# Part of layer 3's edge sort moved on VectorE, from layer 1's graph passes into the loop of layer 1's expert mixture

## Chip, cores and metric

The kernel runs on one core of a Trainium2 chip. The metric is the device time in microseconds (us). Before the change the median of three runs is 3659.58 us, the lowest 3652.49 and the highest 3664.68. The engines are named as in the profile: PE is TensorE, DVE is VectorE, ACT is ScalarE, POOL is GpSimd and SP is SyncE.

## What is computed

Four layers run on 3125 nodes with 256 features and 50000 edges. Each layer is a graph part and then a feed-forward part. Three of these parts touch the change:

```python
# layer 1, graph part: four graph convolutions, one after another
h = relu(gcn_conv(x, src, dst, W1, b1, n)); z = relu(gcn_conv(h, src, dst, W2, b2, n))
h = relu(gcn_conv(z, src, dst, W3, b3, n)); x_hat = gcn_conv(h, src, dst, W4, b4, n)
# layer 1, feed-forward: 16 experts, the two best for each node
topk_vals, topk_idx = top_k(x @ gate_w + gate_b, 2)
moe = sum(softmax(topk_vals) * expert_out[topk_idx]); y = layernorm(x + moe) * gamma + beta
# layer 3, graph part: it needs the edges grouped by key (tile of the target, leading or not)
x = x + L3_gnn(layernorm(x), weight, bias, edge_index, edge_type_8)
```

## The kernel before

The nodes lie in T = 25 tiles of 125 rows. Layer 1's graph part (`layer1_gnn`, L1820) makes four passes over 25 blocks of the edge-count matrix. SP loads a block or finds it resident, ACT casts it to 16 bits (L2007), PE multiplies it (L1924), and DVE scales the product and splits it into parts (L2039 to L2094). After each block DVE calls `sort.step(dve, p * T + j)`, which is one small step of `EdgeSort` (L2127). That class prepares layer 3's edges, in 392 columns by 128 partitions and 30 keys, with a counting sort:

- In pass 0 the keys, their totals and the offsets are made (steps 5 to 14).
- A **rank** (L2256 to L2263) handles one key with four operations on 128x392: a comparison, a scan, a multiply-add and an add into `pos`. Ten ranks run at steps 15 to 24 of pass 0, and twenty at steps 75 to 94, which are 20 of the 25 blocks of pass 3.
- A **tiles** operation (L2252) on 1x420 counts, for one key, which tiles of the sorted table start behind it. The thirty of them run at steps 25 to 54, that is after every block of pass 1 and after the first five of pass 2.
- The **last steps** (L2266 to L2291, at step 96) turn tiles and positions into tables and rows.

`scatter` (L2293) is what uses the rows. POOL runs it only after layer 1.

Beside all this, POOL adds layer 2's edge weights into a matrix in memory, column by column: 391 indirect transfers that add (`add_weight`, L1288, issued at L1296). The first 258 (`BEFORE_EXPERTS`) come before the expert mixture, the others in it and after it. Layer 2 starts with loads from that matrix.

Layer 1's expert mixture (`layer1_ffn`, L2660) sorts the 6250 node-expert pairs into 64 blocks of 128 rows. A barrier (`stage`, L94, its wait at L106) stands ahead of its loop. In the loop POOL gathers the rows of a block (L2787), eight blocks ahead. PE turns them (L2845) and multiplies them twice (L2853, L2876). DVE adds the bias (L2913, the "y add"), and POOL scatters the result (L2801). After 56 of the 64 blocks, all but every eighth, POOL also issues one weight add:

```python
for n in range(SLOTS):
    pool.wait_ge(x_turned, n + 1)
    if n + ROWS < SLOTS + 2:
        gather(n + ROWS)
    pool.wait_ge(y_put, n + 3)
    pool.indirect_dma_start(out=g.moe[:, :], ..., in_=ys[:, n % AHEAD, :], ...)
    if n in beside:
        add_weight(nc, g, pool, BEFORE_EXPERTS + FIRST + beside.index(n))
```

DVE has nothing else in that loop than one addition of beta to all of `X` ahead of the first block (L2905) and the 64 y adds. PE waits at block n for y add n - 2, whose place in PSUM it writes again. The order on every engine is the order in which the code is written.

Of the kernel before, what the change touches and what calls it, by code (L numbers as in the profile page):

```python
# [2126 lines left out]
class EdgeSort:  # L2127
# [3 lines left out]

    KEYED, TOTALS, OFFSETS, RANKS, ROWS = 5, 7, 14, [*range(15, 25), *range(75, 95)], 96

# [6 lines left out]
    def signals(self, ctx):  # L2140
        _, _, sem = bufs(self.nc, ctx, "sort")
        self.cleared, self.loaded, self.blank, self.filled, self.counted, self.summed, self.placed = (
            sem(m) for m in ("cleared", "loaded", "blank", "filled", "counted", "summed", "placed"))

    def rooms(self, sub, sums):
        sb, _, _ = bufs(self.nc, sub, "sort")
        self.raw = sb("raw", [128, 3, ET], I32)
        self.key, self.pos, self.pad = self.g.cell_id, self.g.cell_off, self.g.trash
        self.tmp, self.hot, self.run, self.one = (sb(m, [128, ET]) for m in ("tmp", "hot", "run", "one"))
        self.each = sb("each", [128, 5, ET], BF16)  # L2150
        self.tiles, self.padrow = sb("tiles", [1, ST]), sb("padrow", [128, 1])
        self.leads = self.raw[0:1, :, :].rearrange("p k t -> p (k t)")[:, 0:ST].bitcast(F32)
        self.total, self.nt, self.ends, self.starts, self.off = (
            sb(m, [128, KEYS]) for m in ("total", "nt", "ends", "starts", "off"))
        self.sums = sums

    def load(self, sp, a):
# [9 lines left out]
    def clear(self, dve):  # L2167
# [7 lines left out]
        nc.vector.memset(self.one[:, :], 1.0)  # L2175
        nc.vector.memset(self.tiles[:, :], -1.0)
        dve.drain()
# [19 lines left out]
    def step(self, dve, i):  # L2197
# [40 lines left out]
        if i == self.OFFSETS:  # L2238
# [10 lines left out]
                                           op0=ALU.mult, op1=ALU.add)  # L2249
            dve.drain()  # L2250
        if T <= i < T + KEYS:
            nc.vector.scalar_tensor_tensor(out=self.tiles[:, :], in0=g.iota[0:1, :], scalar=starts[0:1, i - T:i - T + 1],  # L2252
                                           in1=self.tiles[:, :], op0=ALU.is_ge, op1=ALU.add)
# [11 lines left out]
        if i == self.ROWS:  # L2265
# [4 lines left out]
            nc.vector.tensor_scalar(self.leads[:, :], self.leads[:, :], -1.0, 2.0, ALU.mult, ALU.add)  # L2270
            dve.drain()
            nc.vector.tensor_scalar(self.tiles[:, :], self.tiles[:, :], -float(LEADING), None, ALU.add)
            nc.vector.tensor_copy(g.levels[0:1, :], self.leads[:, 0:RING])
            dve.drain()
            nc.vector.tensor_copy(g.kmap[0:1, :], self.tiles[:, :])
            nc.vector.tensor_scalar(tmp[:, :], pos[:, :], 1.0 / 128, -63.5 / 128, ALU.mult, ALU.add)
            dve.drain()
            self.round(dve, tmp[:, :])
            nc.vector.scalar_tensor_tensor(out=pos[:, :], in0=tmp[:, :], scalar=-128.0, in1=pos[:, :],
                                           op0=ALU.mult, op1=ALU.add)  # L2280
# [3 lines left out]
            nc.vector.tensor_scalar(pad[:, :], pad[:, :], self.padrow[:, :], None, ALU.mult)  # L2284
            dve.drain()
            for c in range(EC + 1, ET):
                nc.vector.tensor_scalar(pad[:, c:c + 1], pad[:, c:c + 1], float(128 * (c - EC)), None, ALU.add)
# [371 lines left out]

def layer1_ffn(nc, g, a):  # L2660

# [6 lines left out]
    with ExitStack() as ctx:  # L2668
        sb, ps, sem = bufs(nc, ctx, "f1")
        logits, chosen, weight = sb("logits", [128, T, NE]), sb("chosen", [128, T, 2]), sb("weight", [128, T, 2])  # L2670
        posf = sb("posf", [128, 2 * T])
# [92 lines left out]
        with ExitStack() as sub:  # L2764
# [136 lines left out]
            @block.vector  # L2901
            def _(dve):
                dve.sem_inc(y_put, 2)
                dve.wait_ge(affine_loaded, 32)
                nc.vector.tensor_tensor(g.X[0:P], g.X[0:P], wide(beta[0:P, :], P, T, D), ALU.add)  # L2905
                for i in range(BODIES):
                    for j in range(AHEAD):
                        n = AHEAD * i + j
                        dve.wait_ge(b_loaded[j], (i + 1) * 16)
                        if i:  # L2910
                            dve.wait_ge(stored[j], i * 16 + stored_before[j])
                        dve.wait_ge(y_made, n + 1)
                        nc.vector.tensor_tensor(ys[:, j, :], pY[:, j % 2, 0:D], b[:, j, :], ALU.add).then_inc(y_put, 1)  # L2913

        with ExitStack() as sub:
# [737 lines left out]
def build(nc, a, out):  # L3653
    with ExitStack() as ctx:
        def sb(name, shape, dt=F32):
            return ctx.enter_context(nc.sbuf_tensor(name, shape, dt))
# [52 lines left out]
        sort = EdgeSort(nc, g, keep)  # L3709
        kept = keep.enter_context(ExitStack())  # L3710
        csb, _, _ = bufs(nc, kept, "cells")
        g.cell_id, g.cell_off, g.trash = (csb(m, [128, ET]) for m in ("id", "off", "trash"))
        g.cell_count = csb("count", [128, ET], U16)
# [20 lines left out]
        with ExitStack() as early:  # L3734
            NE, _, F = a["L1_ffn_w1"].shape
            g.w2 = early.enter_context(nc.sbuf_tensor("w2", [128, NE * F // 128 * D], F32))
            layer1_ffn(nc, g, a)
        clear_semaphores(nc, g)
# [31 lines left out]
```

## Time and profile before

| | us |
|---|---|
| median of 3 runs (lowest, highest) | 3659.58 (3652.49, 3664.68) |
| span of the profiled execution | 3782.6 |
| PE busy in it | 2772.2 (73%) |
| POOL busy | 2338.7 (62%) |
| DVE busy | 1733.1 (46%) |
| ACT busy | 916.1 (24%) |
| mean granted TensorE clock | 0.845 |

The profiled execution gives no time but its span, which is 123 us above the median of the runs without a profile. Times in its trace count from the span's start. The part that the change touches lies between 864 us (start of layer 1's pass 0) and 1835 us (the last weight add). A busy share of the whole span says little about it: pass 3 and the expert loop have different bounds.

### The profile page before, as it was taken

To read this page: it belongs to the slowest core of one execution; us is meant where nothing else is said; L and a number is where in the kernel's file an instruction comes from. 1 tells how busy PE (TensorE), PEld (TensorE's weight loads), DVE (VectorE), ACT (ScalarE), POOL (GpSimd) and SP (SyncE) were. 2 spreads that over 40 slices of the span, in tenths; PEclk is the share of its full clock that TensorE was granted. 3 is DMA by queue.
4 is the path that set the end of the run, shared out by engine and by line. 5 is a ranking of instruction groups with operands and counts; after the bars stand their busy time and mean duration, and the time that the engine had idled before them with its cause. 6 is when DMAs were issued, how large, how long until landed. Compare 5 with 4: busy or idle time off the path is not lost.

```text
span 3782.6 us, 57993 instructions
## 1 busy us (share of the span) xinstructions
PE 2772.2 (73%) x20290; PEld 2148.5 (57%) x20291; DVE 1733.1 (46%) x4547; ACT 916.1 (24%) x2203; POOL 2338.7 (62%) x1884
## 2 busy tenths in 40 slices
PE   3778446728989849871699989989996444446897
PEld 2556425627988848761588878855543223225565
DVE  7996765325766650017111122234443444446344
ACT  4654221125674403323111100022110000001121
POOL 6788888887888877778665566610016667661332
PEclk9767677769999859995899999989998767767899
DMA  8655222226785748773445533311236333336342
GB/s 317 185 154 127 1 1 13 9 1 181 168 213 125 158 92 214 205 207 44 112 138 178 200 107 134 104 34 55 67 103 202 95 92 94 92 89 160 78 134 68
DMA packets 286360, 449.09 MB, mean 119 GB/s; under 512 B 167034, under 2 KB 214887, under 8 KB 272124
## 3 DMA queue, kind: packets, MB, share of 16 engines
q1 hardware_dynamic: 121376, 296.50, 24.7%
q0 software_dynamic: 160256, 104.37, 18.0%
q10 hardware_dynamic: 4464, 44.80, 2.9%
q8 instruction: 153, 2.51, 0.3%
q14 instruction: 111, 0.91, 0.1%
HBM read 319.16 MB, written 125.83 MB: 118 GB/s over the span
## 4 chain that ended last, share of the span: by engine, by line
PE 35%; POOL 8%; DVE 8%; another core or an unknown queue 8%; issue 7%; DMA 3%; DVEq 2%; ACT 1%; SPq 1%; POOLq 0%; ACTq 0%
PE g_acc L2405 12%; POOL weight_cells L1296 8%; PE f2m_pR L3137 5%; DVE X L1387 4%; PE f3e_pH L3591 3%; PE f2m_pR L3109 3%; DMA weight_cells<-added_weight,added_row 3%; PE f1e_pH L2853 3%; PE f3e_pY L3600 2%; PE f1e_pY L2876 2%; DVE g3g_hot L1365 2%; PE f2m_pO L3120 1%; PE g3g_pp L1358 1%; PE g_psL L2389 1%
## 5 line engine op out<-in xcount | busy, mean ns | idle before, releaser
L508 POOL DMA_INDIRECT count_cells<-cells_count,added_row x391 | 643.1, 1645 | 155.4 <-issue 130.6
L1296 POOL DMA_INDIRECT weight_cells<-added_weight,added_row x391 | 635.9, 1626 | 139.1 <-issue 113.7
L2405 PE MATMUL g_acc<-g_H,g_blocks 125*125 125x256 f32 x2500 | 565.2, 385 | 38.3 <-DMA g_blocks<-weight_cells 34.8
L2307 POOL DMA_INDIRECT slots_dram<-sort_rec,sort_row x392 | 378.1, 965 | 262.2 <-DMA slots_dram<-sort_rec,sort_row 124.6
L2405 PEld LDWEIGHTS g_acc<-g_H,g_blocks 125*125 125x125 f32 x2500 | 473.2, 191 | 111.3 <-issue 40.0
L1345 POOL DMA_INDIRECT g3a_got<-relations,g3g_idx x316 | 306.2, 969 | 150.0 <-issue 88.7
L1358 PE MATMUL g3g_pp<-g3a_got,g3g_hot 128*125 128x256 f32 x728 | 233.5, 461 | 224.1 <-DVE X L1387 119.6
L1358 PEld LDWEIGHTS g3g_pp<-g3a_got,g3g_hot 128*125 128x125 f32 x728 | 148.7, 223 | 308.9 <-issue 288.8
L1387 DVE TENSOR_TENSOR X<-X,g3g_pp 125x256 f32 x420 | 176.8, 421 | 300.0 <-DMA f_b<-in_L_ffn_b 191.2
L3292 POOL DMA_INDIRECT g3a_got<-relations,g3a_first x48 | 46.5, 968 | 366.8 <-SPq L3071 345.5
L2007 ACT CAST g_blocks<-g_blocks 128x3125 f16<-128x3125 uint16 x85 | 235.7, 2793 | 101.5 <-DMA g_blocks<-count_cells 96.4
L2472 DVE SCALAR_TENSOR_TENSOR g_tmp<-g_acc,dinv,g_b 125x256 f32<-125x256 f32 x50 | 24.2, 484 | 488.4 <-PE g_acc L2405 285.2
L1113 ACT ACTIVATE X<-same_scores 128x128 bf16<-128x128 f32 (+3 forms) x392 | 166.0, 438 | 113.3 <-PE same_scores L1102 93.0
L3137 PE MATMUL f2m_pR<-f2m_w,f2m_tT 128*125 128x512 f32 x400 | 181.4, 607 | 14.5 <-DVE f2m_ys L3244 11.4
L1924 PE MATMUL g_acc<-XN,g_blocks 125*128 125x64 bf16 (+1 forms) x3750 | 173.8, 207 | 8.5 <-issue 6.9
L1924 PE MATMUL g_acc<-parts,g_blocks 125*128 125x128 bf16 (+1 forms) x3750 | 171.0, 206 | 6.9 <-issue 4.5
L1924 PEld LDWEIGHTS g_acc<-XN,g_blocks 125*128 125x128 f16 x3750 | 167.0, 98 | 14.9 <-issue 11.2
L1924 PEld LDWEIGHTS g_acc<-parts,g_blocks 125*128 125x128 f16 x3750 | 164.2, 98 | 12.3 <-issue 7.5
L2853 PE MATMUL f1e_pH<-f1e_xT,f1e_w 128*128 128x128 f32 x1040 | 132.7, 282 | 26.0 <-issue 15.9
L2853 PEld LDWEIGHTS f1e_pH<-f1e_xT,f1e_w 128*128 128x128 f32 x1040 | 125.3, 195 | 41.5 <-issue 25.9
L2913 DVE TENSOR_TENSOR f1e_ys<-f1e_pY,f1e_b 128x256 f32<-128x256 f32 x64 | 27.2, 425 | 258.9 <-PE f1e_pY L2876 146.4
L1100 PE MATMUL same_scores<-edges_other,edges_own 128*128 128x128 bf16 (+3 forms) x392 | 141.0, 374 | 5.4 <-DMA edges_other<-digits_dram 5.4
(777 smaller groups left out, 5305.4 us busy)
## 6 DMA issues: line engine op xcount, KB each, us to landing
g_blocks<-weight_cells SPq DMA_DIRECT2D x49, 1562.5 KB
g_blocks<-count_cells SPq DMA_DIRECT2D x85, 781.2 KB, 14.2
weight_cells<-edges_stripe ACTq DMA_DIRECT2D x25, 1562.5 KB
f1e_w<-in_L_ffn_w SPq DMA_DIRECT2D x68, 512.0 KB
relations<-f2m_ys SPq DMA_DIRECT2D x25, 896.0 KB
f_w<-in_L_ffn_w SPq DMA_DIRECT2D x16, 1024.0 KB
count_cells<-edges_XT POOLq DMA_DIRECT2D x19, 781.2 KB
f1e_b<-in_L_ffn_b SPq DMA_DIRECT2D x68, 128.0 KB
```

What stands on the lines that cost most here:

```text
L508: pool.indirect_dma_start(out=rows, out_offset=bass.IndirectOffsetOnAxis(ap=g.cell_row[:, t:t + 1], axis=0), in_=g.cell_count[:, t:t + 1], ...
L1113: self.nc.scalar.activation(self.same[:, k % self.SAME, 0:n], self.scores[:, k % self.SCORES, 0:n], ACT.Relu, accum_out=self.found[:, k:k ...
L1296: pool.indirect_dma_start(out=rows, out_offset=bass.IndirectOffsetOnAxis(ap=g.cell_row[:, t:t + 1], axis=0), in_=g.cell_weight[:, t:t + 1] ...
L1345: pool.indirect_dma_start(out=ahead.place(j), out_offset=None, in_=table[:, :], in_offset=bass.IndirectOffsetOnAxis(ap=idx[:, n:n + 1], ax ...
L1358: last = nc.tensor.matmul(pp[0:P, n // 2 % BANKS, half], hot[:, n % HOTS, :], ahead.place(j), start=True, stop=True)
L1387: nc.vector.tensor_tensor(part, part, pp[0:P, n // 2 % BANKS, half], ALU.add).then_inc(added if n % 2 else first_added, 1)
L1924: last = nc.tensor.matmul(acc[:, i % ACCS, 0:WIDTH[p]], blocks[0:P, place(p, j), t * P:t * P + 128], part(p, t, k), start=(t == 0 and k == ...
L2007: nc.scalar.copy(blocks[:, at, 0:N], counts[:, at, 0:N]).then_inc(halved, 1)
L2307: pool.indirect_dma_start(out=g.slots_dram[:, :], out_offset=bass.IndirectOffsetOnAxis(ap=self.row[:, c:c + 1], axis=0), in_=self.rec[:, c ...
L2405: last = nc.tensor.matmul(acc[0:P, i % 3, 0:D], blocks[0:P, i % BLOCKS, t * P:(t + 1) * P], H[p][0:P, t, :], start=(t == 0), stop=(t == T ...
L2853: last = nc.tensor.matmul(pH[:, j % 2, f * 128:(f + 1) * 128], w1[:, j % AHEAD, k, f * 128:(f + 1) * 128], xT[:, j % 2, k * 128:(k + 1) * ...
L3137: last = nc.tensor.matmul(pR[0:P, chunk_place(n), :], tT[:, (t - 1) % 3, k, :], w[:, k, 2 * c:2 * c + 2, :].rearrange("p r n -> p (r n)"), ...
```

## The change

Twenty ranks, thirty tiles operations and the last steps leave the DVE code of the four passes and are called in the DVE loop of the expert mixture instead, each after a y add: a tiles operation after each of the blocks 0 to 29, a rank after each of the even blocks 0 to 38, and the last steps, in five pieces, after the blocks 40 to 44. The ten ranks of pass 0 stay. The buffers move with them: at step 14 the 128x392 rooms (`tmp`, `hot`, `run`, `one`) move into `g.slots`, which is free once it has been written out as a blank (`filled`), with a new memset of `one`. `tiles` and `leads` are allocated in the mixture, where `tiles` is set to -1 ahead of the addition of beta. `starts`, `off` and `padrow` become views of `sort.row`. No transfer and no wait of another engine is added or removed.

```diff
-    KEYED, TOTALS, OFFSETS, RANKS, ROWS = 5, 7, 14, [*range(15, 25), *range(75, 95)], 96
+    KEYED, TOTALS, OFFSETS, RANKS = 5, 7, 14, [*range(15, 25), *range(100, 140, 2)]
+    BESIDE, ROWS = 100, 140
...
+    def last_rooms(self, ctx):
+        sb, _, _ = bufs(self.nc, ctx, "sort")
+        self.tiles, self.leads = sb("tiles", [1, ST]), sb("leads", [1, ST])
...
+    def move_rooms(self, dve):
+
+        dve.wait_ge(self.filled, 16)
+        free = self.g.slots[:, :, :].rearrange("p t f -> p (t f)")
+        self.tmp, self.hot, self.run, self.one = (free[:, k * ET:(k + 1) * ET] for k in range(4))
+        self.nc.vector.memset(self.one, 1.0)
+        dve.drain()
...
-        nc.vector.memset(self.tiles[:, :], -1.0)
...
-            dve.drain()
-        if T <= i < T + KEYS:
-            nc.vector.scalar_tensor_tensor(out=self.tiles[:, :], in0=g.iota[0:1, :], scalar=starts[0:1, i - T:i - T + 1],
+            self.move_rooms(dve)
+        if self.BESIDE <= i < self.BESIDE + KEYS:
+            k = i - self.BESIDE
+            nc.vector.scalar_tensor_tensor(out=self.tiles[:, :], in0=g.iota[0:1, :], scalar=starts[0:1, k:k + 1],
                                            in1=self.tiles[:, :], op0=ALU.is_ge, op1=ALU.add)
...
+        if i == self.ROWS + 1:
             nc.vector.tensor_scalar(self.tiles[:, :], self.tiles[:, :], -float(LEADING), None, ALU.add)
...
+        if i == self.ROWS + 2:
             nc.vector.tensor_scalar(tmp[:, :], pos[:, :], 1.0 / 128, -63.5 / 128, ALU.mult, ALU.add)
...
+        if i == self.ROWS + 3:
             nc.vector.scalar_tensor_tensor(out=pos[:, :], in0=tmp[:, :], scalar=-128.0, in1=pos[:, :],
...
+        if i == self.ROWS + 4:
             for c in range(EC + 1, ET):
...
-def layer1_ffn(nc, g, a):
+def layer1_ffn(nc, g, a, sort):
...
+        sort.last_rooms(ctx)
...
                 dve.sem_inc(y_put, 2)
+                nc.vector.memset(sort.tiles[:, :], -1.0)
+                dve.drain()
                 dve.wait_ge(affine_loaded, 32)
                 nc.vector.tensor_tensor(g.X[0:P], g.X[0:P], wide(beta[0:P, :], P, T, D), ALU.add)
...
                         nc.vector.tensor_tensor(ys[:, j, :], pY[:, j % 2, 0:D], b[:, j, :], ALU.add).then_inc(y_put, 1)
+                        sort.step(dve, sort.BESIDE + n)
+                        dve.drain()
...
-            layer1_ffn(nc, g, a)
+            layer1_ffn(nc, g, a, sort)
+        ranked.close()
```

On DVE in pass 1 before, one block's six operations stand between two tiles operations. `parts` and `g_some` belong to the pass, `sort_` to the sort:

```order
L2252 SCALAR_TENSOR_TENSOR sort_tiles<-iota,sort_starts,sort_tiles 1x420
L2053 SCALAR_TENSOR_TENSOR g_some<-g_acc,dinv,g_b 125x64
L2056 TENSOR_SCALAR g_some<-g_some,dinv 125x64
L2039 CAST parts<-g_some 125x64
L2041 TENSOR_TENSOR g_left<-g_some,parts 125x64
L2043 CAST parts<-g_left 125x64
L2045 TENSOR_TENSOR parts<-g_left,parts 125x64
L2252 SCALAR_TENSOR_TENSOR sort_tiles<-iota,sort_starts,sort_tiles 1x420
```

After the change the six operations of a block follow each other directly, in all 25 blocks of pass 1; the last row here begins the next block:

```order
L2053 SCALAR_TENSOR_TENSOR g_some<-g_acc,dinv,g_b 125x64
L2056 TENSOR_SCALAR g_some<-g_some,dinv 125x64
L2039 CAST parts<-g_some 125x64
L2041 TENSOR_TENSOR g_left<-g_some,parts 125x64
L2043 CAST parts<-g_left 125x64
L2045 TENSOR_TENSOR parts<-g_left,parts 125x64
L2053 SCALAR_TENSOR_TENSOR g_some<-g_acc,dinv,g_b 125x64
```

On DVE at the start of the expert loop before, from the branch into it (L2901) on:

```order
L2901 UNCONDITIONAL_BRANCH
L2905 TENSOR_TENSOR X<-X,f_beta 125x6400
L2913 TENSOR_TENSOR f1e_ys<-f1e_pY,f1e_b 128x256 x64
L110 UNCONDITIONAL_BRANCH
L2932 UNCONDITIONAL_BRANCH
L2938 SCALAR_TENSOR_TENSOR XN<-w,f_weight,XN 125x256 x10
```

So the 64 y adds stand there with nothing between them. The same place after the change, where `slots` holds the moved rooms of the sort and `sort_row` the views of it:

```order
L2919 UNCONDITIONAL_BRANCH
L2922 MEMSET sort_tiles 1x420
L2925 TENSOR_TENSOR X<-X,f_beta 125x6400
L2933 TENSOR_TENSOR f1e_ys<-f1e_pY,f1e_b 128x256
L2264 SCALAR_TENSOR_TENSOR sort_tiles<-iota,sort_row,sort_tiles 1x420
L2268 TENSOR_SCALAR slots<-cells_id 128x392
L2270 SCALAR_TENSOR_TENSOR slots<-slots 128x392
L2272 SCALAR_TENSOR_TENSOR slots<-slots,sort_row 128x392
L2275 TENSOR_TENSOR cells_off<-cells_off,slots 128x392
L2933 TENSOR_TENSOR f1e_ys<-f1e_pY,f1e_b 128x256
L2264 SCALAR_TENSOR_TENSOR sort_tiles<-iota,sort_row,sort_tiles 1x420
L2933 TENSOR_TENSOR f1e_ys<-f1e_pY,f1e_b 128x256
```

So a memset stands ahead of the addition to `X`, five operations follow an even block's y add and one an odd block's.

## Rows read from the trace of the kernel before

**Rows 1.** The page: the span, and the chain that ended last, by line.

```profile
span 3782.6 us, 57993 instructions
...
PE g_acc L2405 12%; POOL weight_cells L1296 8%; PE f2m_pR L3137 5%; DVE X L1387 4%; PE f3e_pH L3591 3%; PE f2m_pR L3109 3%; DMA weight_cells<-added_weight,added_row 3%; PE f1e_pH L2853 3%; PE f3e_pY L3600 2%; PE f1e_pY L2876 2%; DVE g3g_hot L1365 2%; PE f2m_pO L3120 1%; PE g3g_pp L1358 1%; PE g_psL L2389 1%
```

**Rows 2.** Windows table: pass 1, pass 2, pass 3, expert loop (cut inside it).

```profile
core 0: us, PE busy (x) PEld busy (x) DVE busy (x) ACT busy (x) POOL busy (x), PEclk, DMA share, GB/s
1003.00:1072.00 69.00, 60.26 (x1866) 56.59 (x1865) 52.12 (x167) 54.38 (x20) 57.72 (x38) 1.00 0.84 215
1077.00:1168.00 91.00, 81.78 (x2046) 71.99 (x2046) 56.18 (x180) 59.55 (x46) 75.31 (x50) 1.00 0.75 180
1168.00:1291.00 123.00, 120.95 (x1954) 116.36 (x1954) 86.75 (x170) 61.21 (x46) 103.78 (x64) 0.99 0.51 100
...
1412.00:1664.00 252.00, 227.12 (x1509) 202.94 (x1508) 24.64 (x58) 83.40 (x290) 193.64 (x166) 0.99 0.79 209
```

**Rows 3.** Timeline, DVE in pass 1: start us, duration us, engine, line, operation.

```profile
1016.53 0.65 DVE L2252 SCALAR_TENSOR_TENSOR sort_tiles<-iota,sort_starts,sort_tiles 1x420 f32<-1x420 f32 x1
...
1019.33 0.65 DVE L2252 SCALAR_TENSOR_TENSOR sort_tiles<-iota,sort_starts,sort_tiles 1x420 f32<-1x420 f32 x1
```

**Rows 4.** Timeline, ACT in pass 1: its last cast of a count block.

```profile
1062.66 2.80 ACT L2007 CAST g_blocks<-g_blocks 128x3125 f16<-128x3125 uint16 x1 [0.70 <-DMA g_blocks<-count_cells]
```

**Rows 5.** Timeline, PE: the last matmuls of pass 1's last block.

```profile
1072.18 0.25 PE L1951 MATMUL g_acc<-g_heavy_rows,heavier_target_hot 128*128 128x64 bf16 x3
```

**Rows 6.** Timeline, DVE in pass 3: one rank and the next block's first operation.

```profile
1200.95 0.36 DVE L2256 TENSOR_SCALAR sort_hot<-cells_id 128x392 f32<-128x392 f32 x1
1201.39 0.98 DVE L2258 TENSOR_TENSOR_SCAN sort_run<-sort_one,sort_hot 128x392 f32<-128x392 f32 x1
1202.44 0.63 DVE L2260 SCALAR_TENSOR_TENSOR sort_run<-sort_run,sort_off,sort_hot 128x392 f32<-128x392 f32 x1
1203.14 0.57 DVE L2263 TENSOR_TENSOR cells_off<-cells_off,sort_run 128x392 f32<-128x392 f32 x1
1204.17 0.29 DVE L2069 COPY g_u<-g_acc 125x128 f32<-125x128 f32 x1 [0.46 <-PE g_acc L1951]
```

**Rows 7.** Timeline, POOL at the expert loop's start.

```profile
1391.63 1.01 POOL L2787 DMA_INDIRECT f1e_xs<-table,f_node  x1 [11.92 <-DVEq L106]
1392.94 6.48 POOL L2787 DMA_INDIRECT f1e_xs<-table,f_node  x1 [0.30 <-issue]
1399.73 0.95 POOL L2787 DMA_INDIRECT f1e_xs<-table,f_node  x1 [0.30 <-issue]
```

**Rows 8.** Timeline, DVE at the expert loop's start.

```profile
1391.75 6.83 DVE L2905 TENSOR_TENSOR X<-X,f_beta 125x6400 f32<-125x6400 f32 x1 [0.42 <-DVEq L106]
...
1417.20 0.42 DVE L2913 TENSOR_TENSOR f1e_ys<-f1e_pY,f1e_b 128x256 f32<-128x256 f32 x1 [4.05 <-PE f1e_pY L2876]
```

**Rows 9.** Timeline, POOL inside the expert loop: one block's three transfers.

```profile
1504.33 0.99 POOL L2787 DMA_INDIRECT f1e_xs<-table,f_node  x1 [0.30 <-PE f1e_pT L2845]
1505.63 0.97 POOL L2801 DMA_INDIRECT moe<-f1e_ys,f_to  x1 [0.30 <-issue]
1506.91 1.61 POOL L1296 DMA_INDIRECT weight_cells<-added_weight,added_row  x1 [0.31 <-issue]
```

**Rows 10.** Timeline, POOL in pass 3, beside the rank of rows 6.

```profile
1199.91 1.54 POOL L1296 DMA_INDIRECT weight_cells<-added_weight,added_row  x1 [0.30 <-issue]
1201.76 1.96 POOL L1296 DMA_INDIRECT weight_cells<-added_weight,added_row  x1 [0.30 <-issue]
```

**Rows 11.** Groups by line, POOL, pass 3 while it holds ranks (1169.5 to 1268 us).

```profile
L1296 POOL DMA_INDIRECT weight_cells<-added_weight,added_row x51 | 83.9, 1645 | 15.6 <-issue 14.0 <-DMA weight_cells<-added_weight,added_row 1.5
```

**Rows 12.** Groups by line, POOL, pass 1 (1003 to 1072 us).

```profile
L1296 POOL DMA_INDIRECT weight_cells<-added_weight,added_row x38 | 60.1, 1581 | 11.6 <-issue 10.7 <-DMA weight_cells<-added_weight,added_row 0.9
```

**Rows 13.** Waits table, POOL in the expert loop (1412 to 1690): us, times, longest.

```profile
POOL moe L2801 <- DVE f1e_ys L2913: 11.9, 11, 1.6
```

**Rows 14.** Timeline, POOL: the last of layer 1's adds.

```profile
1832.96 1.55 POOL L1296 DMA_INDIRECT weight_cells<-added_weight,added_row  x1 [0.30 <-issue]
```

More of the change, by code:

```diff
@@ L2150, in rooms @@
         self.each = sb("each", [128, 5, ET], BF16)
[L2151 to L2154, printed above, removed]
+        self.total, self.nt, self.ends = (sb(m, [128, KEYS]) for m in ("total", "nt", "ends"))
+        free = self.row[:, :].bitcast(F32)
+        self.starts, self.off, self.padrow = free[:, 0:KEYS], free[:, KEYS:2 * KEYS], free[:, 2 * KEYS:2 * KEYS + 1]
         self.sums = sums
+    def move_rooms(self, dve):
[4 more added lines that the diff above has]
+        dve.drain()
     def load(self, sp, a):
@@ L2913, in _ @@
                         nc.vector.tensor_tensor(ys[:, j, :], pY[:, j % 2, 0:D], b[:, j, :], ALU.add).then_inc(y_put, 1)
+                        sort.step(dve, sort.BESIDE + n)
+                        dve.drain()
         with ExitStack() as sub:
@@ L3709, in build @@
         sort = EdgeSort(nc, g, keep)
-        kept = keep.enter_context(ExitStack())
+        ranked = keep.enter_context(ExitStack())
+        csb, _, _ = bufs(nc, ranked, "cells")
+        g.cell_id, g.cell_off, g.trash = (csb(m, [128, ET]) for m in ("id", "off", "trash"))
+        kept = ranked.enter_context(ExitStack())
         csb, _, _ = bufs(nc, kept, "cells")
-        g.cell_id, g.cell_off, g.trash = (csb(m, [128, ET]) for m in ("id", "off", "trash"))
         g.cell_count = csb("count", [128, ET], U16)
```

## Prediction

> **What bounds the kernel now.** I read the chain of the page first. Layer 1's part of it is POOL's column of weight adds, L1296, with 8% of the span, followed by layer 2's g_acc [rows 1]. The last add begins at 1832.96 us [rows 14], and layer 2 begins by loading the matrix that the adds fill. So whatever moves POOL's end moves the time, about us for us. Next I read the windows table by stage, because the change touches three stages with different limits. In pass 1 neither PE (60.26 of 69 us) nor DVE (52.12) is full, in pass 3 PE is (120.95 of 123), and in the expert loop DVE is nearly idle (24.64 of 252) while POOL is not (193.64 busy, and it pays 0.30 of issue ahead of each of its 166 transfers, 50 us more) [rows 2]. Last I read the timelines. In the loop a block costs POOL three transfers, 0.99 + 0.97 + 1.61 us, and three times 0.30, so 4.47 us [rows 9]. The y add waited 4.05 us and took 0.42, so it comes every 4.47 us too [rows 8]. POOL sets the pace in the loop. Ahead of the loop it does not: its first gather waited 11.92 us for the barrier, which DVE ended [rows 7]. So time saved in the passes does reach the loop's start, as long as POOL has its 258 adds done, and time lost on POOL in the loop reaches the end.
>
> **The change, part by part.** The sum is made in the profiled execution, whose span of 3782.6 us is 123 us above the median of the runs; terms of a few us are taken over unscaled.
>
> *Tiles out of pass 1.* A tiles operation costs DVE 0.65 us and about 0.07 behind it. Where DVE runs back to back, a block takes it 1019.33 - 1016.53 = 2.80 us with it and would take 2.08 without [rows 3]. PE needs 60.26 / 25 = 2.41 us a block [rows 2], so DVE would no longer be behind PE. What remains is the count blocks: the last one is cast at 1062.66 + 2.80 = 1065.46 [rows 4], and one block of PE behind that is 1067.87. Before, PE's last block ended at 1072.43 [rows 5], so 4.6 us can be gained at most here. The least is nothing, if PE's end hangs on the casts in a way that these rows don't show. I take -4, nearer to the upper end, since DVE's excess is seen in every block of the first half.
>
> *Tiles out of pass 2.* Five operations, 0.72 us each. PE was busy 81.78 of 91 us and DVE 56.18 [rows 2], so DVE has room: 0, at best -3.6.
>
> *Ranks and last steps out of pass 3.* A rank is 0.36 + 0.98 + 0.63 + 0.57 us and some 0.3 of drains, 2.86 us [rows 6], and twenty leave. But behind one DVE waited 0.46 us for PE [rows 6], and PE idled only 2.05 us of the pass [rows 2]. PE's matmuls hide the ranks: 0, at best -2. POOL's adds lose their stalls here, but POOL then only waits longer than 11.92 us at the barrier.
>
> *The move of the rooms.* One memset on 128x392 in pass 0, of the size of the comparison's 0.36 us, behind a wait for a write that was issued blocks earlier: 0, bounds 0 and +0.7.
>
> *The memset of tiles ahead of the addition to X.* It and its drain start that addition later. An addition of 6.83 us to all of X runs at the loop's start [rows 8], and the second gather beside it took 6.48 us where the next took 0.95 [rows 7]. PE's first block hangs on these gathers. The addition moves by about one operation on one partition, 0.4 us, and the gather with it: +0.4, bounds 0 and +0.7.
>
> *DVE in the loop.* An even block now costs 0.42 + 0.72 + 2.86 = 4.00 us, an odd one 1.14, against 4.47 between y adds. It fits, by half a microsecond: 0. If that cover went, the next y add would be late, and with it POOL's scatter behind it on POOL's queue, then the next weight add.
>
> *POOL beside the ranks.* This is the price that decides. While a rank's last addition ran from 1203.14 to 1203.71 [rows 6], a weight add that began at 1201.76 did not end before 1203.72: it took 1.96 us instead of 1.54 [rows 10]. In pass 3's stretch with twenty ranks the 51 adds took 1645 ns on the mean [rows 11], so 51 x 0.105 = 5.4 us too long, 0.27 us a rank. There POOL began a transfer every 98.5 / 51 = 1.93 us. In the loop it begins three in 4.47, one per 1.49, so there are 1.3 times as many to hit: 0.35 us a rank, 7.0 for twenty. Tiles operations: in pass 1 the 38 adds took 1581 ns [rows 12], 38 x 0.041 = 1.6 us too long for 25 of them, 0.06 each; times 1.3, thirty cost 2.4. The last steps I count as two ranks, 0.7. That is 10.1 us of stalls. POOL also waits in the loop, 11.9 us in 11 waits for a y add [rows 13], around the blocks 0, 8, 16 and so on that have no weight add. Of the twenty ranks five stand at such a block, so I take a quarter off: +7.6. Bounds: 0 if POOL's waits swallow all of it, and 20 x (0.63 + 0.57) = +24 if every rank costs POOL both its operations on two inputs.
>
> **Sum:** -4 + 0.4 + 7.6 = +4.0 us, about **3663.5 us**. A measurement of this kernel tells some 0.3% (11 us) from no change, so this is no change.
>
> **Rivals.**
> *Slower: the stalls lock to the blocks.* In the passes POOL and DVE drift past each other, and 0.27 is a mean over all positions. In the loop the y add follows the gathers that POOL issues, so a rank stands at the same place against POOL's three transfers in each block, and it can be a bad one. If each of twenty ranks costs its last addition, 0.57, and every second tiles operation its whole 0.65, that is 11.4 + 9.8 + 0.7 + 0.4 - 4 = +18, so 3678 us. It decides from about 0.7 us per even block on. For it: the y adds and POOL show the same period [rows 8, 9]. Against it: POOL's slack at every eighth block, and no add in rows 10 lost more than 0.42.
> *Faster: the passes give all and the loop takes nothing.* -4.6 in pass 1, -3.6 in pass 2, -2 in pass 3 and stalls that vanish in POOL's 11.9 us of waits: -10, about 3650 us. For it: the 11.92 us at the barrier lets a gain through. Against it: PE's full pass 3, and that each part must give its upper bound.
> *The move out of the passes is worth nothing.* If pass 1 hangs on its loads (the last cast waited 0.70 us for one [rows 4]), the gain is 0 and the stalls stay: +8, 3667.5 us, still inside what can't be told.
> *Only the comparison stalls POOL.* The addition to X reads two inputs from the core's memory, and the gather beside it was held for 6.48 us [rows 7, 8]; the trace so speaks for stalls by such operations. If they didn't stall POOL in the loop, a rank would hold it only by its comparison, 0.36 us once in 1.49 of POOL's starts and for half of it, 0.04 us: below 1 us for twenty, a sum of -2.7 and 3657 us. The Trainium skill, "SBUF — State Buffer", section "Who interferes with whom", says that an operation with two SBUF inputs takes only the read side of the port that GpSimd shares, and infers that it should not hold up the generation of descriptors, where a fast one-input operation does. By that rule the sum would be this rival's; rows 7 and 8 speak against it here, so I give it little.
>
> **How the numbers follow.** My own case with the last two rivals beside it: 0.60 (forecast 0.47, nothing from the passes 0.08, comparison only 0.05), from 3655 to 3670. Locked stalls: 0.25. All gains: 0.15. The range leaves out about one in ten on each side and goes from 3649, the full gain, to 3679, the locked case. Within 0.3% is 3648.6 to 3670.6, so same is 0.60, slower 0.25 and faster 0.15.
>
> **What would show it.** In the profile after, pass 1 should end about 4 us earlier against pass 0's end, pass 3 should still take 121 us with PE full, and POOL's wait at the barrier should grow from 11.92. In the loop transfers of POOL beside a rank should be 0.3 to 0.5 us longer, ending when a DVE operation ends, and the last add should start about as late as before. The forecast is wrong if the loop grows by more than 15 us, or if its transfers keep 0.99, 0.97 and 1.61 us beside the ranks.

## The result and the profile after

The change makes the kernel a little slower. The median goes from 3655.48 to 3665.16 us (twenty runs each), and the ratio is 1.0023 with a 95% interval of 1.0016 to 1.003. That is 9.7 us by the medians and 8.4 by the ratio (6 to 11 by its interval). It is less than the 0.3% at which the forecast drew its line, but with twenty runs the interval leaves 1 out: it is a small loss, not none. The forecast was 3663.5 us, in a range of 3649 to 3679.

The page after the change, its span and its chain by line:

```profile
span 3664.6 us, 58012 instructions
...
PE g_acc L2422 15%; POOL weight_cells L1296 12%; POOL g3a_got L1345 6%; PE f2m_pR L3159 5%; PE f3e_pH L3613 3%; PE f2m_pR L3131 3%; PE f3e_pY L3622 3%; DMA weight_cells<-added_weight,added_row 2%; PE f2m_pO L3142 1%; DMA g3a_got<-relations,g3g_idx 1%; PE g_psL L2406 1%; PE g3g_pp L1358 1%; POOL moe L2819 1%; POOL f1e_xs L2805 1%; PE f1e_pH L2871 1%
```

POOL's weight adds now hold 12% of the chain, where [rows 1] had 8%. But the span of [rows 1] is 3782.6 us and this one 3664.6, and most of that difference lies behind layer 1, where the change does nothing. The first profiled execution was an unusual one. So the kernel before was profiled once more, and what follows compares with that second execution (span 3652.0 us).

> The kernel before, unchanged, for a second profiled execution: the first one spans 3782.6 us and its stages behind layer 1 can't be set beside those after the change. Theory A (POOL's stalls in the expert loop make the loss): in an ordinary execution the last weight add ends 5 to 10 us earlier than after the change, counted from pass 0's first matmul, and the later stages agree to 1 or 2 us. Theory B (the loss arises behind layer 1): from pass 0's first matmul to the last weight add it takes about 963 us as in the first profile, 6 us more than after the change, and a later stage is some 15 us shorter.

It measured 3653.73 us. From pass 0's first matmul to the end of the last weight add it took 948.7 us, and after the change 957.2: 8.6 us more, as theory A expected, while theory B's 963 did not come again. Behind that add the two executions differ by 3.3 us (1831.4 and 1834.7), more than the 1 or 2 that theory A allowed; in the profiled executions below this stretch goes from 1834 to 1842 us, so a single trace can't place a few us there.

POOL by line over its whole expert loop, from the first gather to the last scatter, in this second execution of the kernel before (columns: instructions | busy us, mean ns | idle ahead of them and what ended it):

```profile
L1296 POOL DMA_INDIRECT weight_cells<-added_weight,added_row x58 | 93.3, 1608 | 17.7 <-issue 16.5 <-DMA weight_cells<-added_weight,added_row 0.9 <-DVE f1e_ys L2913 0.3
L2787 POOL DMA_INDIRECT f1e_xs<-table,f_node x66 | 70.7, 1070 | 24.3 <-issue 18.0 <-DVEq L106 4.5 <-PE f1e_pT L2845 1.2
L2801 POOL DMA_INDIRECT moe<-f1e_ys,f_to x64 | 62.4, 975 | 19.5 <-issue 17.7 <-DVE f1e_ys L2913 1.2 <-PE f1e_pT L2845 0.3
```

The same for the kernel after the change:

```profile
L1296 POOL DMA_INDIRECT weight_cells<-added_weight,added_row x58 | 95.4, 1644 | 17.7 <-issue 17.1 <-DMA weight_cells<-added_weight,added_row 0.6
L2805 POOL DMA_INDIRECT f1e_xs<-table,f_node x66 | 76.3, 1156 | 29.9 <-issue 17.4 <-DVEq L106 10.1 <-PE f1e_pT L2863 2.1
L2819 POOL DMA_INDIRECT moe<-f1e_ys,f_to x64 | 66.6, 1041 | 19.5 <-issue 18.0 <-DVE f1e_ys L2933 1.2 <-DMA weight_cells<-added_weight,added_row 0.3
```

The same 188 transfers took 93.3 + 70.7 + 62.4 = 226.4 us before and 95.4 + 76.3 + 66.6 = 238.3 after: 11.9 us more. The loop, from the first gather's start to the last scatter's end, went from 283.3 to 295.2 us, by the same 11.9. Nothing was absorbed in the loop, since in both kernels POOL idled almost only for issue: it waited 1.2 us for y adds, not the 11.9 of [rows 13]. The gathers grew most, from 1070 to 1156 ns.

Where the loop begins, in the second execution of the kernel before (timeline of POOL):

```profile
1387.18 1.01 POOL L2787 DMA_INDIRECT f1e_xs<-table,f_node  x1 [4.53 <-DVEq L106]
1388.49 6.49 POOL L2787 DMA_INDIRECT f1e_xs<-table,f_node  x1 [0.30 <-issue]
```

And after the change:

```profile
1387.08 1.01 POOL L2805 DMA_INDIRECT f1e_xs<-table,f_node  x1 [10.07 <-DVEq L106]
1388.39 7.08 POOL L2805 DMA_INDIRECT f1e_xs<-table,f_node  x1 [0.30 <-issue]
```

The first gather starts at the same time. POOL waits longer for the barrier, 10.07 instead of 4.53 us, because the passes no longer hold up its adds: from pass 0's first matmul on, the 254 adds ahead of the mixture took 411.8 us before and 405.8 after, with the same idle time between them (97.3 and 97.4). That longer wait is worth nothing by itself. The second gather is held 0.6 us longer, because the memset makes the addition to X start later; this is in the 11.9 us. Behind the loop 2.5 us come back: the 75 adds left there took 150.1 us before and 147.6 after (147.6 to 148.3 in the other kernels below that have 75). So the last add starts at 1828.36 instead of 1819.08 us, 9.3 us later, and the medians differ by 9.7.

How the time is lost, on one block in the loop after the change. DVE behind the y add of an even block (timeline):

```profile
1504.93 0.42 DVE L2933 TENSOR_TENSOR f1e_ys<-f1e_pY,f1e_b 128x256 f32<-128x256 f32 x1 [1.70 <-PE f1e_pY L2894]
1505.27 0.63 DVE L2264 SCALAR_TENSOR_TENSOR sort_tiles<-iota,sort_row,sort_tiles 1x420 f32<-1x420 f32 x1
1505.83 0.45 DVE L2268 TENSOR_SCALAR slots<-cells_id 128x392 f32<-128x392 f32 x1
1506.35 0.97 DVE L2270 TENSOR_TENSOR_SCAN slots<-slots 128x392 f32<-128x392 f32 x1
1507.40 0.63 DVE L2272 SCALAR_TENSOR_TENSOR slots<-slots,sort_row 128x392 f32<-128x392 f32 x1
1508.10 0.57 DVE L2275 TENSOR_TENSOR cells_off<-cells_off,slots 128x392 f32<-128x392 f32 x1
```

POOL at the same time:

```profile
1505.10 0.99 POOL L2805 DMA_INDIRECT f1e_xs<-table,f_node  x1 [0.30 <-issue]
1506.40 1.71 POOL L2819 DMA_INDIRECT moe<-f1e_ys,f_to  x1 [0.30 <-issue]
1508.41 1.74 POOL L1296 DMA_INDIRECT weight_cells<-added_weight,added_row  x1 [0.31 <-issue]
```

The gather at 1505.10 began inside the y add and ahead of the tiles operation, and took its usual 0.99 us. The scatter at 1506.40 began just inside the scan (1506.35 to 1507.32) and ended 0.79 us behind the scan's end: 1.71 us instead of the 0.97 of [rows 9]. The add at 1508.41 began beside the last addition and lost 0.13.

### The profile page after: what moved, and what is told of

Read it like the earlier page. It is cut to its first block, busy times and chain, and to the rows that moved or that the text cites. A ratio compares the mean times of both kernels' runs of the same rounds, so it can differ in the third digit from the quotient of the medians.

```text
span 3664.6 us, 58012 instructions
## 1 busy us (share of the span) xinstructions
PE 2872.4 (78%) x20242; PEld 2162.1 (59%) x20291; DVE 1725.1 (47%) x4548; ACT 917.5 (25%) x2203; POOL 2344.5 (64%) x1884
## 4 chain that ended last, share of the span: by engine, by line
PE 36%; POOL 22%; issue 8%; DMA 5%; DVE 2%; ACT 1%; SPq 1%; POOLq 0%; DVEq 0%; ACTq 0%
PE g_acc L2422 15%; POOL weight_cells L1296 12%; POOL g3a_got L1345 6%; PE f2m_pR L3159 5%; PE f3e_pH L3613 3%; PE f2m_pR L3131 3%; PE f3e_pY L3622 3%; DMA weight_cells<-added_weight,added_row 2%; PE f2m_pO L3142 1%; DMA g3a_got<-relations,g3g_idx 1%; PE g_psL L2406 1%; PE g3g_pp L1358 1%; POOL moe L2819 1%; POOL f1e_xs L2805 1%; PE f1e_pH L2871 1%
## 5 line engine op out<-in xcount | busy, mean ns | idle before, releaser
L2422 PE MATMUL g_acc<-g_H,g_blocks 125*125 125x256 f32 x2500 | 555.4, 381 | 32.6 <-DMA g_blocks<-weight_cells 32.6
L1358 PE MATMUL g3g_pp<-g3a_got,g3g_hot 128*125 128x256 f32 x728 | 347.7, 597 | 80.1 <-DMA g3a_got<-relations,g3g_idx 52.3
L1358 PEld LDWEIGHTS g3g_pp<-g3a_got,g3g_hot 128*125 128x125 f32 x728 | 161.9, 266 | 265.7 <-DMA g3a_got<-relations,g3g_idx 230.4
L1924 PEld LDWEIGHTS g_acc<-XN,g_blocks 125*128 125x128 f16 x3750 | 167.6, 99 | 11.3 <-issue 7.7
L2894 PE MATMUL f1e_pY<-w,f1e_hT 128*128 x512 | 124.4, 387 | 14.3 <-DVE f1e_ys L2933 12.2
L2871 PEld LDWEIGHTS f1e_pH<-f1e_xT,f1e_w 128*128 128x128 f32 x1040 | 128.1, 195 | 11.9 <-issue 8.9
L3416 ACT COPY f3g_xT<-f3g_psT 128x250 f32<-128x250 f32 x25 | 9.2, 368 | 497.1 <-PE f3g_psT L3394 497.0
```

Of the source, the lines that this page charges most:

```text
L1358: last = nc.tensor.matmul(pp[0:P, n // 2 % BANKS, half], hot[:, n % HOTS, :], ahead.place(j), start=True, stop=True)
L1924: last = nc.tensor.matmul(acc[:, i % ACCS, 0:WIDTH[p]], blocks[0:P, place(p, j), t * P:t * P + 128], part(p, t, k), start=(t == 0 and k == ...
L2422: last = nc.tensor.matmul(acc[0:P, i % 3, 0:D], blocks[0:P, i % BLOCKS, t * P:(t + 1) * P], H[p][0:P, t, :], start=(t == 0), stop=(t == T ...
L2871: last = nc.tensor.matmul(pH[:, j % 2, f * 128:(f + 1) * 128], w1[:, j % AHEAD, k, f * 128:(f + 1) * 128], xT[:, j % 2, k * 128:(k + 1) * ...
```

## The experiments

Three theories stood at the start: A, POOL's stalls in the loop make the loss; B, it arises behind layer 1; C, it comes from the new places of the buffers. All ratios are against runs of the kernel before on the same chip, and the loop's length is taken from the profiled execution of each kernel.

**Tiles alone.** Edit against the kernel after:

```diff
-    KEYED, TOTALS, OFFSETS, RANKS = 5, 7, 14, [*range(15, 25), *range(100, 140, 2)]
+    KEYED, TOTALS, OFFSETS, RANKS = 5, 7, 14, [*range(15, 25), *range(75, 95)]
```

> Only the thirty tiles operations and the last steps are moved; the twenty ranks stay in pass 3. Theory A: pass 1 gains its 4 us, tiles and last steps cost POOL about 3, so the time is within 2 us of before. Theory B (a later stage, whatever moved): as after the change, +8 to +10 us. Theory C (addresses of buffers): as after, +8 to +10 us.

Ratio 1.0005 (0.9996 to 1.0014), so no change that can be told. The loop is 286.6 us, 3.3 more than before. The time is what theory A expected, though not for its reason, since pass 1 did not gain 4 us (see the next section). B and C fall.

**Ranks alone.** Edit against the layout kernel below: the steps of the ranks and the steps on positions go into the loop, and the tiles stay in the passes.

```diff
-    KEYED, TOTALS, OFFSETS, RANKS = 5, 7, 14, [*range(15, 25), *range(75, 95)]
-    BESIDE, ROWS = 25, 96
+    KEYED, TOTALS, OFFSETS, RANKS = 5, 7, 14, [*range(15, 25), *range(200, 240, 2)]
+    BESIDE, ROWS, LOOP, PLACES = 25, 96, 200, 240
...
+                        sort.step(dve, sort.LOOP + n)
+                        dve.drain()
```

> Only the twenty ranks and the steps on positions are moved; the tiles operations stay in passes 1 and 2. Theory A: no gain in pass 1, the ranks cost POOL 7 to 12 us in the loop, so +7 to +14 us over before. Theory B: +8 to +10. Theory C: +8 to +10.

Ratio 1.0023 (1.0014 to 1.0032): the loss of the whole change. The loop is 289.6 us, 6.2 more than before, inside the 5 to 12 us of that interval. Counted from pass 0's first matmul the last add came only 4.0 us later; the rest isn't placed.

**The buffers alone.** Edit against the kernel after: the steps go back into the passes, and `tiles` with its memset too.

```diff
-    KEYED, TOTALS, OFFSETS, RANKS = 5, 7, 14, [*range(15, 25), *range(100, 140, 2)]
-    BESIDE, ROWS = 100, 140
+    KEYED, TOTALS, OFFSETS, RANKS = 5, 7, 14, [*range(15, 25), *range(75, 95)]
+    BESIDE, ROWS = 25, 96
...
-                        sort.step(dve, sort.BESIDE + n)
-                        dve.drain()
```

> All operations stay where they were before; only the buffers lie as after the change (rooms moved into slots at step 14, three small ones as views, cells kept through the mixture). Theory A: within 1 us of before. Theory B: within 1 us of before too, if it is the moved work that acts on a later stage. Theory C: the whole +8 to +10 us.

Ratio 1.0 (0.9991 to 1.0009), loop 283.4 us. Where these buffers lie costs nothing that can be told. `tiles` and `leads` lie as before here; the kernel with the tiles alone has them moved too, and lost nothing that can be told either.

**Does POOL's end set the time?** Edit against the kernel after:

```diff
-BEFORE_EXPERTS = 258
+BEFORE_EXPERTS = 263
```

> The kernel after the change with 263 instead of 258 weight adds ahead of the expert mixture. After the change POOL stands 10.1 us at the barrier ahead of the loop; five adds of 1.85 us fit in there and leave POOL's end. Theory A (POOL's own work from the loop to its last add sets the end, the stalls cost 12 us there): the last add ends 9 us earlier and the time falls by 7 to 9 us, to within 3 us of before. If POOL's end didn't set layer 2's start, the time would stay at +8 to +10 us.

Ratio 1.0006 (0.9997 to 1.0015), 1.9 us over before: the five adds at the barrier won back most of the loss, and the last add ended 9.2 us earlier, counted from pass 0's first matmul. So POOL's adds are what sets layer 2's start, and the wait at the barrier that the change had made longer can be used.

**The same with the tiles alone.** The same edit on the first of these kernels.

> Only the tiles operations and the last steps moved, ranks in pass 3, and 263 adds ahead of the mixture. In the run with the tiles moved POOL stood some 10 us at the barrier and lost 3 us in the loop. Theory A: 6 to 8 us faster than before, about 3648 us. Rival (the adds that are pulled forward collide with the count blocks' loads or hold back the barrier): within 2 us of before, or slower.

Ratio 1.0 (0.9991 to 1.0009): the rival's number. Timeline of POOL ahead of the loop in this run:

```profile
1340.92 1.54 POOL L1296 DMA_INDIRECT weight_cells<-added_weight,added_row  x1 [5.37 <-DMA weight_cells<-added_weight,added_row]
...
1385.88 7.66 POOL L1296 DMA_INDIRECT weight_cells<-added_weight,added_row  x1 [0.31 <-issue]
1393.84 1.54 POOL L1296 DMA_INDIRECT weight_cells<-added_weight,added_row  x1 [0.30 <-issue]
1395.68 1.01 POOL L2805 DMA_INDIRECT f1e_xs<-table,f_node  x1 [0.30 <-issue]
```

The barrier opened as early as with the tiles alone, so it wasn't held back. But the 10 us at the barrier, which the expectation took from one execution of the kernel with the tiles alone, were not there: POOL had waited 5.37 us for the landing of earlier adds, which that execution had not at this place. So two adds were still to come when the barrier opened. The first of them began beside the addition to X and took 7.66 us, and the first gather came at 1395.68, where it came at 1387.08 after the change. What the adds won at the end was paid ahead of the loop.

**Which operations hold POOL?** Two kernels keep the whole sort in the passes and add scratch work to the loop, which the outputs don't use. Edit of the first against the layout kernel, behind the y add (the comparison and the scan of a rank):

```diff
+                        if n % 2 == 0 and n < 40:
+                            dve.drain()
+                            nc.vector.tensor_scalar(sort.hot[:, :], sort.key[:, :], float(10 + n // 2), None, ALU.is_equal)
+                            dve.drain()
+                            nc.vector.tensor_tensor_scan(sort.run[:, :], sort.one[:, :], sort.hot[:, :], 0.0, ALU.mult, ALU.add)
+                            dve.drain()
```

> Everything of the sort where it was before, buffers as after the change; in the expert loop, behind the y adds of blocks 0, 2, ... 38, twenty copies of a rank's first half on scratch: the comparison on one input and the scan. Theory S (operations that read two inputs from the core's memory hold POOL's transfers, the scan not, the comparison little): loop 1 to 2 us longer than the 283.4 without them. Rival by the rule of the port's two sides (a fast operation on one input holds POOL, one on two inputs does not hold the issue of a transfer): nearly the whole 6 us that the twenty ranks cost alone.

The second has the other half instead (the multiply-add and the addition):

```diff
+                            nc.vector.scalar_tensor_tensor(out=sort.run[:, :], in0=sort.one[:, :], scalar=1.0, in1=sort.hot[:, :],
+                                                           op0=ALU.add, op1=ALU.mult)
+                            dve.drain()
+                            nc.vector.tensor_tensor(sort.tmp[:, :], sort.pos[:, :], sort.run[:, :], ALU.add)
```

> The same with twenty copies of a rank's second half on scratch: the multiply-add and the addition, each with two inputs from the core's memory. Theory S: loop 4 to 6 us longer than 283.4. Rival: less than 1 us longer.

The loops are 287.4 us (4.0 longer than with the buffers alone; ratio 1.0017, 1.0008 to 1.0027) and 286.3 us (2.9 longer; 1.0016, 1.0006 to 1.0025). Both theories missed. The first half, on DVE:

```profile
1502.21 0.50 DVE L2932 TENSOR_SCALAR slots<-cells_id 128x392 f32<-128x392 f32 x1
1502.78 0.97 DVE L2934 TENSOR_TENSOR_SCAN slots<-slots 128x392 f32<-128x392 f32 x1
```

and on POOL beside it:

```profile
1502.84 2.34 POOL L1296 DMA_INDIRECT weight_cells<-added_weight,added_row  x1 [0.30 <-issue]
```

The add began just inside the scan and took 2.34 us: from the scan's end at 1503.75 it still needed 1.43, nearly the 1.61 of an add from its start. So the scan, which reads two inputs as well, holds POOL. Two more places of this trace, DVE's operation and POOL's transfer beside it, tell of the comparison and of the scan without a multiply-add behind it:

```profile
1493.61 0.36 DVE L2932 TENSOR_SCALAR slots<-cells_id 128x392 f32<-128x392 f32 x1
1493.70 1.76 POOL L1296 DMA_INDIRECT weight_cells<-added_weight,added_row  x1 [0.31 <-issue]
...
1557.39 0.97 DVE L2934 TENSOR_TENSOR_SCAN slots<-slots 128x392 f32<-128x392 f32 x1
1557.44 1.71 POOL L2817 DMA_INDIRECT moe<-f1e_ys,f_to  x1 [0.31 <-DMA weight_cells<-added_weight,added_row]
```

The add at 1493.70 ended 1.49 us behind the comparison's end: an operation on one input holds POOL too, for what is left of its 0.36 us. The scatter at 1557.44 took the 1.71 us of the one above, by the scan alone.

The second half, on DVE:

```profile
1500.40 0.57 DVE L2932 SCALAR_TENSOR_TENSOR slots<-slots 128x392 f32<-128x392 f32 x1
1501.04 0.57 DVE L2935 TENSOR_TENSOR slots<-cells_off,slots 128x392 f32<-128x392 f32 x1
...
1507.73 0.57 DVE L2932 SCALAR_TENSOR_TENSOR slots<-slots 128x392 f32<-128x392 f32 x1
```

and on POOL:

```profile
1501.12 1.97 POOL L1296 DMA_INDIRECT weight_cells<-added_weight,added_row  x1 [0.31 <-issue]
...
1507.89 1.27 POOL L2803 DMA_INDIRECT f1e_xs<-table,f_node  x1 [0.30 <-issue]
```

The add at 1501.12 began inside the addition and lost 0.36, the gather at 1507.89 inside the multiply-add and lost 0.28. Both halves together cost 6.9 us, the twenty real ranks 6.2.

The loops of all these kernels (twelve traces, the first execution left out) agree on when a transfer is held. 132 transfers began at least 0.1 us inside a DVE operation other than a y add that still had 0.2 us or more to run, with no next operation overlapping it. The gathers and scatters ended 0.78 to 0.89 us behind that operation's end, the adds 1.42 to 1.51, whatever the operation: addition to X, tiles, comparison, scan, multiply-add or addition. 129 transfers began beside a y add alone, which reads one of its inputs from PSUM; none took over 0.02 us more than its usual time. And of 159 transfers that were running before the first such operation began, 157 kept theirs to 0.06 us.

**The largest holder moved out of the way.** The addition of beta to X, ahead of the loop instead of in it, on the kernel before:

```diff
                 nc.vector.tensor_scalar(away[:, :], g.iota[:, 0:SLOTS], first[:, :], None, ALU.add)
+                dve.wait_ge(affine_loaded, 32)
+                nc.vector.tensor_tensor(g.X[0:P], g.X[0:P], wide(beta[0:P, :], P, T, D), ALU.add)
...
-                dve.wait_ge(affine_loaded, 32)
-                nc.vector.tensor_tensor(g.X[0:P], g.X[0:P], wide(beta[0:P, :], P, T, D), ALU.add)
```

> The kernel before, with the addition of beta to X moved from the start of the expert loop into the stage ahead of it, where DVE waits 14 us for PE. The addition is the largest single holder of POOL: the second gather took 6.5 us beside it. Theory A: ahead of the barrier it holds one weight add for about 5.5 us instead; POOL stands 4.5 us at the barrier there, so some 1 us of it shows, the loop gets 5.5 us shorter, and the time falls by 4 to 5 us. Rival (the start of the loop is set by PE's first block or by a load, not by the gathers): no change.

Ratio 0.9986 (0.9978 to 0.9995), 3653.86 us: 5.1 us faster than before by the ratio, 3.6 by the medians, and the only version here that beats both kernels. POOL in this run:

```profile
1381.04 7.04 POOL L1296 DMA_INDIRECT weight_cells<-added_weight,added_row  x1 [0.30 <-issue]
...
1395.78 1.54 POOL L1296 DMA_INDIRECT weight_cells<-added_weight,added_row  x1 [0.30 <-issue]
1397.63 1.01 POOL L2789 DMA_INDIRECT f1e_xs<-table,f_node  x1 [0.31 <-issue]
1398.94 0.98 POOL L2789 DMA_INDIRECT f1e_xs<-table,f_node  x1 [0.30 <-issue]
```

The second gather took 0.98 us. One add ahead of the barrier is held instead, 7.04 us, and POOL no longer waits at the barrier at all, so part of the 5.5 us is paid there.

The same edit on the kernel after:

> The kernel after the change with the same move. POOL stands 10.1 us at the barrier after the change, so the held add is covered whole and the loop loses its 6 us at the start: 6 us below the time after the change, +3 to +4 us over before. If the passes' relief were worth nothing at all to POOL, it would be only 4 to 5 us below.

Ratio 1.0012 (1.0002 to 1.0022), against 1.0023 without the edit: 4 us less instead of the 6 expected, in intervals that allow both; the last add ended 6.0 us earlier, counted from pass 0's first matmul. And with the tiles alone and two more adds ahead (edits as above, `BEFORE_EXPERTS = 260`):

> Only the tiles operations and last steps moved, beta early, and 260 weight adds ahead of the mixture. Theory A: from the run with the tiles moved (last add as in the kernel before, to 1 us) take 6 us for beta and 3.7 us for two adds that fit at the barrier: 8 to 9 us faster than before. Rival: as in the run with 263 adds, an add is held beside another DVE operation just ahead of the barrier and the loop starts later: within 4 us of before.

Ratio 1.0004 (0.9995 to 1.0013). The rival's range holds, though not for its reason: no add missed the barrier. Counted from pass 0's first matmul, the last add ended 1.8 us ahead of the kernel before, where 8 to 9 were expected. Against the kernel with the tiles alone the first gather came 2.8 us later (516.9 to 514.1), and the loop got 4.4 us shorter instead of 6. Behind the loop the two adds that had been moved ahead were worth almost nothing: POOL waited 6.4 us there for the landing of earlier adds, where with the tiles alone it waited 3.4, so 73 adds took 147.7 us and 75 had taken 148.2.

## Why the prediction was right, and where not

The forecast was a net of terms, +4.0 us. It came out at 8 to 10, inside the range and on the side of the sign that it gave, but below its bound for slower. The mechanism that it gave for the loss, POOL's transfers held beside DVE's operations in the loop, is what the runs show. Two of its terms were wrong, and both made the loss too small; that the time still lies in the range owes something to the range's width. Term by term:

**Tiles out of pass 1, forecast -4: this step failed.** The prediction took PE's end to hang on DVE, which ran back to back [rows 3]. Without the tiles DVE is free and the pass is as long. The last matmuls of pass 1's last block, in the second execution of the kernel before and then after the change:

```profile
1070.19 0.25 PE L1951 MATMUL g_acc<-g_heavy_rows,heavier_target_hot 128*128 128x64 bf16 x3
```

```profile
1070.33 0.25 PE L1951 MATMUL g_acc<-g_heavy_rows,heavier_target_hot 128*128 128x64 bf16 x3
```

From pass 0's first matmul that is 198.5 us before and 197.9 after. ACT and DVE in pass 1 (1000 to 1072 us), before:

```profile
L2007 ACT CAST g_blocks<-g_blocks 128x3125 f16<-128x3125 uint16 x20 | 54.4, 2796 | 4.1 <-DMA g_blocks<-count_cells 4.1
```

```profile
L2053 DVE SCALAR_TENSOR_TENSOR g_some<-g_acc,dinv,g_b 125x64 f32<-125x64 f32 x24 | 6.8, 284 | 2.7 <-PE g_acc L1951 1.0
```

After the change:

```profile
L2007 ACT CAST g_blocks<-g_blocks 128x3125 f16<-128x3125 uint16 x20 | 54.7, 2797 | 5.8 <-DMA g_blocks<-count_cells 5.8
```

```profile
L2053 DVE SCALAR_TENSOR_TENSOR g_some<-g_acc,dinv,g_b 125x64 f32<-125x64 f32 x25 | 7.1, 283 | 20.6 <-PE g_acc L1951 20.3
```

DVE now waits 20.3 us for PE where it waited 1.0, and twenty casts of 2.80 us with their waits for loads fill ACT from the first to the last as before, 54.7 + 5.8 us. A cast of 2.80 us a block is just DVE's 2.80 of [rows 3], so ACT with its loads may be the second bound. That is argued from the equal pace and was not tested; PE's last block ended 6.4 us behind the last cast's end before and 5.3 after. DVE took that block up at 1073.87, 3.4 us behind PE's end. The only wait of PE for it that the trace shows from there on is one of 1.45 us at the opening of pass 2, for the last parts; after the change there is none. From pass 0's first matmul to the loop's first gather it took 515.2 us before and 514.4 after; over the five kernels with the tiles in the passes and the five without them where the barrier set that start, the means are 515.7 and 514.4. That is 1.3 us, with a scatter of 4 among like kernels. It was the rival "the move out of the passes is worth nothing", at 3667.5 us, that came nearest. It was priced with what the rows showed and given too small a chance; that loads bind pass 1, its condition, is not shown.

**Passes 2 and 3, forecast 0: right.** From ACT's cast of `g_heavy_rows` for pass 2 to the loop's first gather it took 310.9 us before and 312.3 after.

**Memset ahead of the addition, forecast +0.4: right,** the second gather took 7.08 instead of 6.49 us.

**Stalls in the loop, forecast 10.1 less a quarter: size right, the quarter wrong.** The loop grew by 11.9 us, 0.6 of it for the memset, so they came to 11.3. Tiles, last steps and memset alone cost 3.3 (forecast 3.1 + 0.4), ranks and steps on positions alone 6.2 (7.0 and a part of the 0.7), all together 2.4 more than the sum of the two. That 2.4 is hardly clear of the scatter: the kernel after with 263 adds, which has the same loop, took 293.3 us for it instead of 295.2. The price itself rested on a reading that was wrong in part. The add of [rows 10] that was put down to the rank's last addition began inside the scan of [rows 6], which ended at 1202.37, and ended 1.35 us behind it; the mean loss per rank had the scan and the comparison in it all the same, but the bound of +24 left both out. The quarter was taken off for waits that only the first profiled execution had [rows 13]. In the second, POOL's transfers take the same time, but the waits are gone. Had the two wrong steps been left out, the sum would have been 0 + 0.4 + 10.1 = 10.5, near the 9.7 of the medians, though it has no term for the 2.5 us that came back behind the loop.

**Rival "the stalls lock to the blocks":** the price per even block, 11.9 / 20 = 0.6 us with the tiles, stayed under the 0.7 from which it was to decide. Fixed places do show in the trace after the change, but cheap ones: six scatters began 0.33 to 0.34 us inside a rank's addition and lost 0.11 to 0.14 each.

**Rival "only the comparison stalls POOL":** wrong. The scratch pair without any comparison lengthened the loop by 2.9 us. The comparison does hold POOL as well, for its own 0.36 us at most. The Trainium skill, "SBUF — State Buffer", section "Who interferes with whom", says that a VectorE instruction with two SBUF inputs contends with a GpSimd instruction that reads SBUF, and infers that it leaves descriptor generation alone. An indirect transfer is held by such an operation in all of these runs, by up to 6.1 us in the last add but one ahead of the loop in the kernel with the tiles alone and 263 adds. The first half of that rule may be what acts here, with the transfer's list of rows read from SBUF; the traces don't show which access waits.

## What to carry to other kernels

Before moving work from one engine's queue into a stage where that engine is idle, ask which engine bounds the stage, and whether the moved operations hold it: here a nearly idle DVE took 12 us from POOL. An engine that runs back to back need not be the bound: look at when the engine behind it ends, and for a second engine of the same pace, before counting its relief. Take waits only from an execution whose time is that of the ordinary runs.

## What the hardware showed that was not expected

A transfer issued by POOL that begins while DVE runs an operation on the core's memory waits until that operation ends, and then takes nearly its whole time: 2.34 instead of 1.61 us for an add beside the scan, 1.76 beside a comparison on one input, 1.97 beside an addition. A tiles operation on a single partition held gathers in the same way, and a y add with one input in PSUM held none of 129. A transfer that is already running when the operation begins keeps its time, with 2 exceptions in 159. And two executions of one kernel, 3782.6 and 3652.0 us long, had the same transfer times on POOL to 0.1 us in the loop, while POOL's waits for y adds differed by 10.7 us.
